# Layer 0 attention in a two-layer fp32 kernel: the carried state as 32x32 blocks of the heads

## The reference

```python
q, k, v = split_heads(xn @ Wqkv + bqkv)            # 16 heads, hd = 32
def body(S, (qb, kb, vb)):                          # S: per head 32 x 32
    scores  = einsum('bhid,bhjd->bhij', qb, kb) * intra_decay
    o_intra = einsum('bhij,bhjd->bhid', scores, vb)
    o_inter = einsum('bhid,bhde->bhie', qb * q_decay, S)
    S_new   = blk_decay * S + einsum('bhjd,bhje->bhde', kb * k_decay, vb)
    return S_new, o_intra + o_inter
s = concat_heads(o) @ Wout + bout
x = x + s * silu(ffn(xn))                           # then layer 1
```

## Time and profile before

| | us |
|---|---|
| median of 3 runs | 3000.16 (2997.89 to 3001.02) |
| the profiled execution, its own time | 2999.55 |
| its span, first to last instruction | 2997.8 |
| TensorE busy | 2848.9 (95%) |
| VectorE busy | 1857.0 (62%) |
| ScalarE busy | 1291.0 (43%) |
| GpSimd busy | 1416.7 (47%) |
| mean granted clock of TensorE | 0.984 |

### The profile page before, as it was taken

One profiled execution on the slowest core, in us unless ns is written; L12 is line 12 of the kernel. 1 busy time (PEld: TensorE's weight loads), 2 busy tenths in 40 slices (PEclk: granted clock), 3 DMA queues, 4 the chain that ended last, 5 costly groups with the idle time before them and its releaser, 6 DMA issues. The chain is left out here.

```text
span 2997.8 us, 54358 instructions
## 1 busy us (share of the span) xinstructions
PE 2848.9 (95%) x19392; PEld 2011.7 (67%) x19392; DVE 1857.0 (62%) x2721; ACT 1291.0 (43%) x2021; POOL 1416.7 (47%) x1003
## 2 busy tenths in 40 slices
PE   6999999799999997799999999999999789999999
PEld 5878787688888886455555555555555368888887
DVE  5656766577777764666666666666666744444444
ACT  3221111266666663355555555555555522222222
POOL 2003555122333222377777777777777732222222
PEclk9999999999999998799999999999999999999999
DMA  3221211122232224122222222222222332222221
GB/s 127 88 61 49 65 61 53 36 71 85 84 105 84 84 90 160 58 71 71 71 71 72 71 71 71 71 71 71 72 78 77 121 127 85 85 89 86 91 84 49
DMA packets 124567, 238.99 MB, mean 80 GB/s; under 512 B 13440, under 2 KB 48384, under 8 KB 124416
## 3 DMA queue, kind: packets, MB, share of 16 engines
q1 hardware_dynamic: 120896, 235.32, 23.2%
q10 hardware_dynamic: 3520, 1.46, 0.2%
HBM read 178.02 MB, written 58.72 MB: 79 GB/s over the span
## 5 line engine op out<-in xcount | busy, mean ns | idle before, releaser
L1330 DVE TENSOR_REDUCE l_attn_maxima<-l_attn_ps_max 128x2 f32<-128x1024 f32 x502 | 613.6, 1222 | 234.2 <-PE l_attn_ps_max L1455 230.2
L1301 POOL TENSOR_TENSOR l_attn_summed<-l_attn_summed,stage 128x1024 f32<-128x1024 f32 x248 | 586.0, 2397 | 52.9 <-ACT stage L1239 52.9
L1239 ACT ACTIVATE stage<-l_attn_ps_sc 128x1024 f32<-128x1024 f32 x512 | 497.8, 1029 | 157.3 <-PE l_attn_ps_sc L1443 136.0
L1301 POOL TENSOR_TENSOR l_attn_summed<-stage 128x1024 f32<-128x1024 f32 x124 | 293.4, 2388 | 240.1 <-ACT stage L1239 240.1
L1702 POOL TENSOR_TENSOR l_ffn_ht_lo<-stage,l_ffn_ht_hi 128x512 fp32r<-128x512 f32 x88 | 114.0, 1296 | 413.9 <-ACT l_ffn_ht_hi L1723 413.9
L62 PE MATMUL l_attn_ps_prep<-l_w_tile,l_x_tiles 128*128 (+1 forms) x1440 | 287.1, 348 | 6.3 <-DVE l_attn_qk_lo L1324 2.0
L62 PEld LDWEIGHTS l_attn_ps_prep<-l_w_tile,l_x_tiles 128*128 128x128 f32 x1440 | 248.9, 190 | 39.3 <-issue 29.4
L1465 PE MATMUL l_attn_ps_y<-stage,l_attn_v 128*32 128x512 f32 x2048 | 273.6, 606 | 1.1 <-ACT stage L1239 1.1
L71 PE MATMUL l_ffn_ps_fc<-l_w_tile 128*128 128x512 f32 x1024 | 268.1, 405 | 6.7 <-DVE l_w_tile L865 5.0
L71 PEld LDWEIGHTS l_ffn_ps_fc<-l_w_tile 128*128 128x128 f32 x1024 | 184.6, 190 | 41.7 <-issue 5.5
L71 PE MATMUL l_ffn_ps_out<-l_ffn_t_proj,l_ffn_ht_hi 128*128 128x512 f32 x512 | 206.9, 404 | 0.0
(11 more groups left out here) (270 smaller groups left out, 6328.6 us busy)
## 6 DMA issues: line engine op xcount, KB each, us to landing
l_x_tiles<-xt_chunks SPq DMA_DIRECT2D x160, 512.0 KB, 3.7
xt_chunks<-l_w_tile SPq DMA_DIRECT2D x32, 512.0 KB, 4.7
l_attn_xin<-in_x SPq DMA_DIRECT2D x32, 256.0 KB, 4.3
l_attn_piece<-in_w_fcT SPq DMA_DIRECT2D x16, 512.0 KB, 4.3
s<-l_attn_s_sb SPq DMA_DIRECT2D x32, 256.0 KB, 2.2
l_attn_piece<-in_w_projT SPq DMA_DIRECT2D x16, 512.0 KB, 3.9
l_ffn_xa<-in_x SPq DMA_DIRECT2D x32, 256.0 KB, 2.7
l_ffn_xb<-in_x SPq DMA_DIRECT2D x32, 256.0 KB, 2.9
```

The source lines that it names most:

```text
L1239: act.activation(probs[kt % RING][:, hs, :], ps_sc[:, hs, :], ACT.Exp, scale=ATT_SCALE).then_inc(exp_done, 1)
L1301: pool.tensor_tensor(total[:, hs, :], old[:, hs, :], probs[kt % RING][:, hs, :], ALU.add).then_inc(added, 1)
L1330: dve.tensor_reduce(maxima[b][:, j, PAIR * hp:PAIR * hp + PAIR, half:half + 1], pair, AX.X, ALU.max).then_inc(max_read, 1)
```

## The change

The state becomes `[P, GROUPS, HD]`: partition 32h + d, group g and column e hold the state of head (g, h), so the blocks between different heads are neither kept nor computed.

- **State update**: 16 matmuls instead of 4. Each has one head's 32 columns of `k_dec` as weights (all 128 rows) and that head's 32 columns of v as moving operand, and writes 32 partitions by 32 columns. The wait before it is `state_ready` at c instead of `st_step` at 2c - 1.
- **Inter products**: 16 matmuls instead of 4, each in a tile of 32 rows and 32 columns on the diagonal of the array (rows and columns 32h), with 128 tokens moving; all 16 write the bank `ps_o`.
- **Order**: the wait for the four masks (`masked_ready`) stands behind the inter products instead of before them.
- **VectorE**: two steps on 128x128 elements (`state_kept` = old state times keep and decay; new state = update times keep plus `state_kept`) instead of three on 128x512. The first doesn't wait for the update.
- **GpSimd**: `own_head` goes, and with it one memset and two selects in tick 0; VectorE's two memsets of the states are a quarter as large.

```diff
-                pool.memset(own_head[:, :, :], 1.0).then_inc(iotas, 1)
...
-                v = own_head[:, :, :].rearrange("p g (h e) -> p g h e", h=HPG)
-                pool.affine_select(out=v, in_=v, compare_op=ALU.is_ge, fill=0.0, base=0,
...
-                pool.affine_select(out=v, in_=v, compare_op=ALU.is_ge, fill=0.0, base=HD - 1,
...
                 if live(c, CHUNKS):
+                    kp = keep[:, bass.ds(c, 1)] if not isinstance(c, int) else keep[:, c:c + 1]
+                    need(dve, state_ready, c)
+                    dve.scalar_tensor_tensor(out=state_kept[:, :, :], in0=state[b][:, :, :], scalar=kp,
+                                             in1=blk_decay[:, :].rearrange("p (g a) -> p g a", a=1).to_broadcast([P, GROUPS, HD]),
+                                             op0=ALU.mult, op1=ALU.mult).then_inc(st_step, 1)
                     need(dve, upd_done, c + 1)
-                    dve.scalar_tensor_tensor(out=state_new[:, :, :], in0=ps_state[:, :, :], scalar=kp, in1=own_head[:, :, :],
-                                             op0=ALU.mult, op1=ALU.mult).then_inc(st_step, 1)
-                    need(dve, state_ready, c)
                     need(dve, o_done, c)
-                    dve.scalar_tensor_tensor(out=state[1 - b][:, :, :], in0=state[b][:, :, :], scalar=kp,
...
-                    need(dve, st_step, 2 * c + 2)
-                    dve.tensor_tensor(state[1 - b][:, :, :], state[1 - b][:, :, :], state_new[:, :, :],
-                                      ALU.add).then_inc(state_ready, 1)
+                    need(dve, st_step, c + 1)
+                    dve.scalar_tensor_tensor(out=state[1 - b][:, :, :], in0=ps_state[:, :, :], scalar=kp, in1=state_kept[:, :, :],
+                                             op0=ALU.mult, op1=ALU.add).then_inc(state_ready, 1)
...
-                    need(pe, st_step, 2 * c - 1)
+                    need(pe, state_ready, c)
                     for g in range(GROUPS):
-                        gs = slice(P * g, P * g + P)
-                        mm = pe.matmul(ps_state[:, g, :], k_dec[q][:, gs], qkv[q][:, 2 * DIM + P * g:2 * DIM + P * g + P],
-                                       start=True, stop=True)
+                        for h in range(HPG):
+                            own, v = slice(P * g + HD * h, P * g + HD * h + HD), 2 * DIM + P * g + HD * h
+                            mm = pe.matmul(ps_state[HD * h:HD * h + HD, g, :], k_dec[q][:, own], qkv[q][:, v:v + HD],
+                                           start=True, stop=True, skip_group_check=True)
                     mm.then_inc(upd_done, 1)
...
+                    for g in range(GROUPS):
+                        for h in range(HPG):
+                            r = slice(HD * h, HD * h + HD)
+                            pe.matmul(ps_o[r, g, :], state[q][r, g, :], q_dec[q][r, g, :], start=(g == 0), stop=False,
+                                      skip_group_check=True)
                     need(pe, masked_ready, HPG * c + HPG)
-                    for g in range(GROUPS):
-                        pe.matmul(ps_o[:, g, :], state[q][:, g, :], q_dec[q][:, g, :], start=(g == 0), stop=False,
-                                  skip_group_check=True)
```

More of the change, by code:

```diff
@@ L98, in layer0_attention @@
         blk_decay = sb("blk_decay", [P, GROUPS])
-        own_head = sb("own_head", [P, GROUPS, P])
         keep = sb("keep", [P, CHUNKS])
@@ L125, in layer0_attention @@
         masked = two("masked", [P, HPG, GROUPS, P])
-        state = two("state", [P, GROUPS, P])
-        state_new = sb("state_new", [P, GROUPS, P])
+        state = two("state", [P, GROUPS, HD])
+        state_kept = sb("state_kept", [P, GROUPS, HD])
         ot_hi, ot_lo = two("ot_hi", [P, GROUPS, P], F32R), two("ot_lo", [P, GROUPS, P], F32R)
@@ L133, in layer0_attention @@
         ps_score = [ps_q, ps_k, ps_qt, ps_kt]
-        ps_state = ps("ps_state", [P, GROUPS, P])
+        ps_state = ps("ps_state", [P, GROUPS, HD])
         ps_o = ps("ps_o", [P, GROUPS, P])
@@ L223, in masks @@
                 pool.iota(left[:, :], [[0, 1]], base=P, channel_multiplier=-1, allow_small_or_imprecise_dtypes=True).then_inc(iotas, 1)
-                pool.memset(own_head[:, :, :], 1.0).then_inc(iotas, 1)
                 pool.memset(keep[:, :], 1.0).then_inc(iotas, 1)
-                pool.wait_ge(iotas, 6)
+                pool.wait_ge(iotas, 5)
                 pool.memset(keep[:, CPB - 1::CPB], 0.0).then_inc(masks_made, 1)
-                v = own_head[:, :, :].rearrange("p g (h e) -> p g h e", h=HPG)
-                pool.affine_select(out=v, in_=v, compare_op=ALU.is_ge, fill=0.0, base=0,
-                                   pattern=[[0, GROUPS], [-HD, HPG], [0, HD]], channel_multiplier=1).then_inc(iotas, 1)
-                pool.wait_ge(iotas, 7)
-                pool.affine_select(out=v, in_=v, compare_op=ALU.is_ge, fill=0.0, base=HD - 1,
-                                   pattern=[[0, GROUPS], [HD, HPG], [0, HD]], channel_multiplier=-1).then_inc(masks_made, 1)
             def slope_masks():
@@ L384, in tick @@
                     dve.wait_ge(decays, HEADS + GROUPS + 2)
-                    dve.wait_ge(masks_made, 3)
+                    dve.wait_ge(masks_made, 2)
                 if isinstance(t, int) and t == 0:
@@ L435, in tick @@
                 if live(c, CHUNKS):
+                    kp = keep[:, bass.ds(c, 1)] if not isinstance(c, int) else keep[:, c:c + 1]
[3 more added lines that the diff above has]
+                                             op0=ALU.mult, op1=ALU.mult).then_inc(st_step, 1)
                     need(dve, upd_done, c + 1)
-                    kp = keep[:, bass.ds(c, 1)] if not isinstance(c, int) else keep[:, c:c + 1]
-                    dve.scalar_tensor_tensor(out=state_new[:, :, :], in0=ps_state[:, :, :], scalar=kp, in1=own_head[:, :, :],
-                                             op0=ALU.mult, op1=ALU.mult).then_inc(st_step, 1)
-                    need(dve, state_ready, c)
                     need(dve, o_done, c)
-                    dve.scalar_tensor_tensor(out=state[1 - b][:, :, :], in0=state[b][:, :, :], scalar=kp,
-                                             in1=blk_decay[:, :].rearrange("p (g a) -> p g a", a=1).to_broadcast([P, GROUPS, P]),
-                                             op0=ALU.mult, op1=ALU.mult).then_inc(st_step, 1)
-                    need(dve, st_step, 2 * c + 2)
-                    dve.tensor_tensor(state[1 - b][:, :, :], state[1 - b][:, :, :], state_new[:, :, :],
-                                      ALU.add).then_inc(state_ready, 1)
+                    need(dve, st_step, c + 1)
+                    dve.scalar_tensor_tensor(out=state[1 - b][:, :, :], in0=ps_state[:, :, :], scalar=kp, in1=state_kept[:, :, :],
+                                             op0=ALU.mult, op1=ALU.add).then_inc(state_ready, 1)
                     need(dve, ot_hi_ready, c + 1)
```

## The result

The changed kernel takes 2989.28 us (median of 9 runs, 2985.79 to 2994.31); the kernel before, run beside it, 3000.61 us (9 runs, 2997.89 to 3005.51). The ratio is 0.9961 with a 95% interval of 0.9952 to 0.9970: 11.3 us faster between the medians; 2988.6 us was forecast, with 2985 to 2993 as its bounds. The profiled execution has a span of 2986.0 us against 2997.8.

What follows compares the result with a forecast made beforehand. The stage was taken to run at TensorE's pace. Update 5.8, late ticks 5.7, tick 1 1.0, tables 0.3, less 1.9 in early ticks: 10.9 us off 2999.55 gives 2988.6, bounds 2985 to 2993, range with rivals 2984 to 3004.5.

Steps and rivals of the forecast that it cites:

- The inter products: Tiled, between output projection and intra products: 0.32 + 0.81 + 0.20 = 1.33 us; early ticks lose 0.12, late gain 0.38.
- The rival that row tiles share a bank: Inter product tiles writing `ps_o` run one by one, 3.5 us instead of 0.81 a tick: 3075 us; chance 0.10.
- r: Time of one round of four state update tiles with 32 columns moving, taken as 0.03 to 0.04 us.
- The rival of a small tile at the price of a large one: State update with r = 0.11: 9.6 us lost instead of 5.8 gained, 3004.0 us; chance 0.18 including anything between.
- The wait that takes its place: V waits for K's evacuation instead of the update, starting at 1.25 us; 0.20 us gained in 29 ticks, 5.8.
- The formula: After the tiled update, V could start 0.88 + 8r us after K's last start.
- the mask cover: Masks done 0.58 us after the output projection's last start, 0.75 before the intra products, so not late again.
- my two gains of a late tick: In ticks 15 to 29, 0.38 us from the order and 0.20 from the update, added up.
- VectorE: Two steps on a quarter of the elements, each 0.17 to 0.74 us, free 1.3 us or more; worth nothing.
- The start: Tick 0's tables: two selects and a memset leave GpSimd, the last `wqkv_lo` slice arrives sooner; 0.3 us gained.
- Tick 11: The shorter update gives nothing here, as V already stood 3.1 us for K's evacuation.
- the prediction's third rival: Later stages shift against TensorE's clock drops, up to 5 us either way, gain given back: 2991 to 2995; chance 0.12.

Runs made afterwards that it cites:

- the second experiment: The kernel before with only the state update in 16 tiles of 32 columns, order and VectorE's three steps kept: 2999.23 us, ratio 0.9989.
- the order alone: The kernel before with only the wait for the masks moved behind the inter products: 2991.05 us beside 3001.51, ratio 0.9965.
- the update twice: The changed kernel with each of the 16 state update tiles computed twice in a row: one execution alone, 2994.59 us.
- the full inter products: The kernel before with update in tiles and mask wait moved behind inter products, these full 128x128, VectorE's three large steps kept: 2987.87 us, ratio 0.9949.
- the fourth experiment: The changed kernel with TensorE's wait for K's evacuation moved behind the projection of V: 2982.53 us, ratio 0.9932.

## Why the prediction was right, point by point

The steps against the two profiles, from one start of the state update to another:

| stretch | before | after | gain | forecast |
|---|---|---|---|---|
| start to tick 1 | 39.33 | 39.40 | -0.1 | 0.3 |
| tick 1 | 16.62 | 15.28 | 1.3 | 1.2 |
| ticks 2 to 10 | 149.71 | 148.98 | 0.7 | 0.7 |
| tick 11 | 21.35 | 23.11 | -1.8 | -0.1 |
| ticks 12 to 14 | 49.89 | 49.59 | 0.3 | 0.2 |
| ticks 15 to 29 | 256.93 | 247.85 | 9.1 | 8.7 |
| ticks 30, 31 | 27.13 | 27.16 | 0.0 | 0.0 |
| all behind | 2436.8 | 2434.7 | 2.2 | 0 |

**The inter products** came out to the hundredth: 415.73 to 416.05 is 0.32, the row of 1.07 puts its first and last start 0.80 apart, and 417.05 is 0.20 behind that last start, 1.32 us against 1.33 forecast. The step from 32x32 tiles to column tiles, which no row showed, costs what the nearest row did. **The rival that row tiles share a bank** falls with the same row: sixteen tiles in four row groups write one bank, four at a time, in 1.07 us and not in 3.5. The rule of the Trainium skill ("TensorEngine Tiling (Array Packing)", PSUM Pressure), that different row tiles cannot access one bank at the same time, doesn't bind on the diagonal, where each tile has partitions of its own; other layouts weren't tried.

**The update** has the r that was argued for: eight rounds spread over 0.26 us, 7r + 0.04, so r = 0.031. The rival of a small tile at the price of a large one falls, and with it, across tiles, the rule of the Trainium skill of some 60 cycles for each ("TensorEngine Tiling (Array Packing)", Instruction Overhead). **The wait that takes its place** was named rightly: V starts 1.25 us after K's last start in the rows above, 0.05 behind the evacuation, and without that wait 1.15. The formula had said 0.88 + 8 x 0.031 = 1.13. Five of the ticks are written out and not looped. In four of them (1, 2, 3 and 30) V's second start comes 1.64 to 1.67 us after K's last, so these gain 0.12 to 0.15 and not 0.20; in tick 31 nothing changed, as forecast.

**The step that was wrong and did no harm**: the mask cover. I wrote that the masks would be done 0.58 us after the output projection and leave 0.75 us; it is 0.79, with 0.53 left. I had let them move with V. They don't: with V 0.2 us earlier the norm only stands longer for GpSimd. The norm's group from 270 to 500 us, in the kernel before (L420) and in the changed one (L412):

```profile
L420 DVE TENSOR_SCALAR l_attn_xn<-l_attn_xin,l_attn_mean_var,l_attn_rstd 128x512 f32<-128x512 f32 x13 | 15.5, 1189 | 0.0
L412 DVE TENSOR_SCALAR l_attn_xn<-l_attn_xin,l_attn_mean_var,l_attn_rstd 128x512 f32<-128x512 f32 x14 | 19.7, 1407 | 0.0
```

1.19 us has become 1.41, against the 0.54 us of the kernels in which GpSimd waits for the norm. So my two gains of a late tick, 0.38 for the order and 0.20 for the update, aren't independent: the update alone gives a late tick nothing (the second experiment), and only behind the moved wait its 0.20 appear. The sum of a late tick held because the change has both. The same fault sits under "VectorE": I put each new step at 0.17 to 0.74 us; `state_kept` takes 2.17 in a late tick, as the row above shows. That VectorE's steps are worth nothing was right.

**The start** was mis-sized, 0.3 forecast and -0.1 found. The first projection starts 1.14 us earlier (20.27 against 21.41), and the last slice takes 1.76 us as forecast; but the clock rises at 26.2 us instead of 25.0 (until then matmuls of 512 columns start 0.43 us apart, from then on 0.23). The low stretch is 2.3 us longer, and V of tick 0 starts at 29.64 us against 29.67. **Tick 11** lost 1.8 us where 0.1 was forecast. V starts 4.45 us behind the update's first start instead of 4.19: its wait is longer, 4.0 us instead of 3.1, mostly because the update is shorter. The other 1.5 us are the clock: its low stretch lasts 6.8 us instead of 3.4, and TensorE works through 5.8 us of it behind V's first start instead of 2.9. **Behind the stage** 2.2 us were won without an edit; this part lasts 2434.7 to 2440.8 us in all profiles here. Part of it is the prediction's third rival, working the other way: TensorE runs at its lower level for 94.6 us there after the change and for 97.5 before, and over the eleven profiles (93 to 107 us) more of it mostly goes with a longer part. So of the 11.8 us between the two profiles, 9.6 are seen in the stage up to the last update, where some 11 were forecast; without tick 11 it would be 11.4.

The steps of the ticks are therefore right, and that the total came within 0.7 us of the forecast is luck: what the start and tick 11 lost is nearly what came in behind the stage, and the nine runs of the changed kernel alone spread over 8.5 us.

**What stays open**: how much of tick 11's longer low clock is the change's doing. It was 6.8 us in four of the other kernels with the late stall, and 3.4 in two (the order alone, and the update twice). The two groups differ in V's wait: 3.8 to 4.3 us in the former and the changed kernel, 3.1 to 3.6 in the latter and the kernel before. These are one profile of each kernel, and nothing was varied to test it. Also open is the changed kernel with the wait for the masks back in front of its tiled inter products: no run shows it, and that the moved wait pays rests on the order alone and on the full inter products.

## What to carry to other kernels

Ask of a late wait what its chain hangs on before adding gains up: a shorter step in front of it may only lengthen the wait, and moving independent work ahead of it pays at once. Small tiles paid here where the moving operand shrank (the update), not where only rows or columns of the array were left out (the inter products). When a step becomes shorter, look at the waits written behind it: one of them is often placed earlier than what it protects.

## What the runs showed of the hardware

**GpSimd and VectorE hold each other up, with a sharp edge.** In a late tick of the changed kernel GpSimd's first weight step starts at 427.50 and VectorE's norm 1.72 us later. The norm then ends 0.28 us behind GpSimd's step, in each of ticks 15 to 29 (starts 1.71 to 1.77 us apart). With V 0.1 us earlier (the fourth experiment) it starts 1.63 to 1.67 us after it and isn't held at all. First the changed kernel, then that one:

```profile
427.50 2.85 POOL L242 TENSOR_SCALAR l_attn_below<-l_attn_piece,l_attn_limit 128x1024 bf16<-128x1024 f32 x1
429.22 1.41 DVE L412 TENSOR_SCALAR l_attn_xn<-l_attn_xin,l_attn_mean_var,l_attn_rstd 128x512 f32<-128x512 f32 x1
...
419.02 3.10 POOL L242 TENSOR_SCALAR l_attn_below<-l_attn_piece,l_attn_limit 128x1024 bf16<-128x1024 f32 x1
420.69 0.54 DVE L412 TENSOR_SCALAR l_attn_xn<-l_attn_xin,l_attn_mean_var,l_attn_rstd 128x512 f32<-128x512 f32 x1
```

Instead GpSimd's step is 0.2 us longer, 3.10 against 2.85. The Trainium skill ("SBUF — State Buffer", Who interferes with whom) calls the port pair of the two an exclusive lock, and its Terms say it is held for the full instruction and the loser fully blocks. The held norms agree; the norm that runs in the middle of a GpSimd step doesn't. What decides between 1.67 and 1.71 us wasn't tried.

**Changes of tile shape.** A step into or out of tiles cost 0.09 to 0.10 us over the plain distance of starts: 0.32 us instead of 0.23 from a matmul of 512 columns, 0.20 instead of 0.11 from one of 128. Between two tiled shapes it was 0.20 us too (416.85 to 417.05). Back in full matmuls the second start came 0.34 us behind the first instead of 0.23, 0.1 more; that this is a load of weights which isn't hidden is a guess.

**A wait in looped and in written-out code.** In the changed kernel V starts 0.05 us after the evacuation it waits for in looped ticks and 0.15 in written-out ones, though there its second matmul follows after 0.31 instead of 0.34. Net 0.06 us, for the same wait; the cause is not known.
